# Filling the dummy rows of all later stages in one run during the attention, with a new order of every engine's steps

## The reference

```python
x = x + 0.5 * _L0_ffn_ref(_layernorm(x))     # 8 experts, 128 -> 512 -> 128, gelu, the expert with the top score
x = x + _L0_attn_ref(_layernorm(x))          # conv, then q, k, v with cumulative means, then a 4x MLP with gelu
x = x + 0.5 * _L0_ffn_ref(_layernorm(x))     # the same 8 experts again
x = x + 0.5 * _L1_ffn_ref(_layernorm(x))     # 16 experts, 128 -> 512 -> 128, relu, at most C tokens each
x = x + _L1_attn_ref(_layernorm(x))          # state = a * state + x W_b ; y = layernorm(state W_c)
x = x + 0.5 * _L1_ffn_ref(_layernorm(x))     # the same 16 experts again

# _L1_ffn_ref, its core
C = int(1.25 * T / E)
logits = tokens @ gate_w.T
probs = softmax(logits); expert_idx = argmax(probs)
locations = cumsum(one_hot(expert_idx)) - 1
mask = one_hot(expert_idx) * (locations < C)
dispatch = einsum('tec,td->ecd', sec_mask, tokens)
h = relu(einsum('ecd,edh->ech', dispatch, w1))
ans = einsum('tec,ecd->td', probs * sec_mask, einsum('ech,ehd->ecd', h, w2))
```

## Time and profile before

| | us |
|---|---|
| median of 3 executions | 671.9 (671.17 to 674.94) |
| the profiled execution | 672.23 |
| its span | 670.8 |
| TensorE busy | 617.6 (92%) |
| GpSimd busy | 367.2 (55%) |
| VectorE busy | 448.8 (67%) |
| ScalarE busy | 323.5 (48%) |

### The profile page before, as it was taken

One profiled execution on the slowest core, in us unless ns is written; L12 is line 12 of the kernel. 1 busy time (PEld: TensorE's weight loads), 2 busy tenths in 40 slices (PEclk: granted clock), 3 DMA queues, 4 the chain that ended last, 5 costly groups with the idle time before them and its releaser, 6 DMA issues.

```text
span 670.8 us, 13130 instructions
## 1 busy us (share of the span) xinstructions
PE 617.6 (92%) x3651; PEld 476.8 (71%) x3651; DVE 448.8 (67%) x1882; ACT 323.5 (48%) x1037; POOL 367.2 (55%) x377
## 2 busy tenths in 40 slices
PE   7688899999999999999999799999988987999996
PEld 5547899887867767998998545766744875477773
DVE  5745457886999899854555415778737983477774
ACT  2123558659776555445554105455615731365661
POOL 0647755455220365677557762577760366356776
PEclk8599999999999899999999589999999985999999
DMA  9866676316104032877783514254684411544330
GB/s 266 311 212 194 187 213 202 105 49 201 54 0 83 10 91 61 267 211 201 211 272 99 178 68 104 81 151 141 133 217 142 148 56 51 154 132 142 99 104 15
DMA packets 87031, 94.19 MB, mean 140 GB/s; under 512 B 12156, under 2 KB 65439, under 8 KB 86704
## 3 DMA queue, kind: packets, MB, share of 16 engines
q1 hardware_dynamic: 74400, 74.46, 39.3%
q0 software_dynamic: 10880, 15.07, 6.7%
q10 hardware_dynamic: 1680, 3.82, 1.7%
HBM read 64.42 MB, written 33.76 MB: 146 GB/s over the span
## 4 chain that ended last, share of the span: by engine, by line
PE 63%; DVE 10%; DMA 8%; POOL 6%; issue 5%; ACT 3%; SPq 3%; ACTq 0%; DVEq 0%
PE ps L835 10%; PE ps L827 10%; PE ps L907 6%; PE ps L900 6%; PE ps L882 4%; PE ps L932 4%; PE ps L784 4%; PE ps L745 4%; POOL y L1624 3%; PE ps L849 3%; PE ps L875 3%; POOL xs L1620 2%; PE ps L945 2%; PE ps L817 2%; DMA X<-y 1%
## 5 line engine op out<-in xcount | busy, mean ns | idle before, releaser
L1620 POOL DMA_INDIRECT xs<-X,IDX x128 | 125.8, 982 | 102.9 <-issue 64.1
L1513 ACT ACTIVATE ht<-ps,CL 128x128 f32<-128x128 f32 x336 | 93.0, 379 | 84.6 <-PE ps L827 84.4
L1624 POOL DMA_INDIRECT y<-yt,xi x84 | 83.1, 989 | 48.9 <-DVE yt L1253 33.5
L827 PE MATMUL ps<-xt,w1s 128*128 128x128 f32 x672 | 86.3, 277 | 1.8 <-DVE xt L1247 0.8
L835 PE MATMUL ps<-W,ht 128*128 (+1 forms) x672 | 85.0, 277 | 2.1 <-ACT ht L1513 1.9
L835 PEld LDWEIGHTS ps<-W,ht 128*128 128x128 f32 x672 | 80.0, 192 | 4.4 <-issue 4.2
L827 PEld LDWEIGHTS ps<-xt,w1s 128*128 128x128 f32 x672 | 80.0, 192 | 3.8 <-DVE xt L1247 2.4
L1611 POOL TENSOR_TENSOR sma<-sma,MH 128x4 f32<-128x4 f32 (+1 forms) x24 | 30.6, 1278 | 71.4 <-DVE sma L962 65.1
L932 PE MATMUL ps<-MT,KC 128*128 128x512 f32 x118 | 58.2, 648 | 1.6 <-DVE IDX L1227 1.2
L1570 ACT ACTIVATE hb<-ps 128x320 f32<-128x320 f32 x64 | 26.7, 428 | 51.1 <-PE ps L900 50.8
L1563 ACT ACTIVATE w1s<-x,SE 128x128 f32<-128x128 f32 (+1 forms) x66 | 27.4, 483 | 43.7 <-DVE SE L1356 43.6
(11 more groups left out here) (214 smaller groups left out, 1309.7 us busy)
## 6 DMA issues: line engine op xcount, KB each, us to landing
w1s<-in_w SPq DMA_DIRECT2D x84, 256.0 KB
W<-in_w1x SPq DMA_DIRECT2D x17, 512.0 KB, 4.9
wx<-in_w1x SPq DMA_DIRECT2D x15, 512.0 KB, 4.9
X<-y SPq DMA_DIRECT2D x24, 256.0 KB, 4.7
xs<-ZX SPq DMA_DIRECT2D x32, 185.0 KB
xi<-xs SPq DMA_DIRECT2D x84, 66.0 KB, 3.0
x<-xs SPq DMA_DIRECT2D x22, 148.0 KB, 2.2
xs<-ZB SPq DMA_DIRECT2D x2, 1320.0 KB, 8.5
```

The lines of the kernel that those rows point to most:

```text
L827: r = e.matmul(ps[TILE_BANKS[i % n]][:, c * P:(c + 1) * P], W1[i % NW1][:, c * P:(c + 1) * P], XTT[i % NX][:, :], start=True, stop=True)
L1513: r = e.activation(HT[i % NHT][:, c, :], ps[TILE_BANKS[i % len(TILE_BANKS)]][:, c * P:(c + 1) * P], ACT.Gelu, bias=CL[:, bass.ds(r0 * 4 + ...
L1620: return e.indirect_dma_start(dst, bass.IndirectOffsetOnAxis(ap=IDX[:, n:n + 1], axis=0), X[:, n, 0:w], None, bounds_check=hi, oob_is_err= ...
L1624: return e.indirect_dma_start(dst, bass.IndirectOffsetOnAxis(ap=ix, axis=0), src, None, bounds_check=hi_home, oob_is_err=False, engine_sem ...
```

## The change

`FILL_AFTER` lets all eleven fills go out once one, two or three chunks have left the attention, and SyncE's list has them in one row ahead of the loads of the second layer's first tile. All other lists are written in a new order too. TensorE's list loses three `heat` steps (10 to 12) and three `warm` steps (28, 42 and 58). No other step is added or removed.

```diff
-FILL_AFTER = [("aout", 1 + n // 2) for n in range(len(FILL_GROUPS))] + [("aout", n) for n in (3, 3, 4, 4)] + [("edown", n) for n in (2, 4, 6, 8)]
+FILL_AFTER = [("aout", 1) for n in FILL_GROUPS] + [("aout", n) for n in (2, 2, 2, 2, 3, 3, 3, 3)]
...
     "sp": """
...
-tw.36 tw.37 tw.38 tw.39 tw.40 yload.3 yload.4 yload.5 yload.6 yload.7 fill.0 fill.1 fill.2 fill.3 fill.4 tw.41 fill.5 tload.41 tload.42 tload.43
...
+tw.36 tw.37 tw.38 tw.39 tw.40 yload.3 yload.4 yload.5 yload.6 yload.7 wload.0 fill.0 fill.1 fill.2 fill.3 fill.4 fill.5 fill.6 fill.7 fill.8 fill.9
+fill.10 tw.41 tload.41 tload.42 tload.43 tload.44 tload.45 tload.46 tw.42 tw.43 tw.44 tw.45 tload.47 tload.48 tload.49 tw.46 tw.47 tload.50 tw.48
```

More of the change, by code:

```diff
@@ L228 @@
-eup.49 eup.50 eup.51 eback.11 eturn.13 edown.12 eturn.14 eup.52 eup.53 eup.54 eup.55 eback.12 eup.56 eup.57 eturn.15 edown.13 eup.58 eup.59 eup.60
-eback.13 edown.14 eup.61 eup.62 eup.63 eback.14 edown.15 eback.15 warm.29 warm.30 warm.31 warm.32 warm.33 warm.34 warm.35 warm.36 warm.37 warm.38
-warm.39 warm.40 warm.41 warm.42 rturn.0 rB.0 rturn.1 rturn.2 rB.1 rB.2 rC1.0 rC1.1 rC2.0 rC1.2 rC2.1 rC2.2 pturn.21 rturn.3 rturn.4 pscore.24 pturn.22
-pturn.23 rB.3 rB.4 qrank.8 pscore.25 rturn.5 pscore.26 rC1.3 rC1.4 rturn.6 qrank.9 rC2.3 rC2.4 rB.5 rB.6 pturn.24 qrank.10 pturn.25 pscore.27
@@ L232 @@
-pscore.28 rC1.5 rturn.7 rC1.6 qrank.11 rC2.5 qrank.12 rC2.6 rB.7 pturn.26 pturn.27 pscore.29 rC1.7 pscore.30 qrank.13 rC2.7 qrank.14 pturn.28
-pscore.31 qrank.15 warm.43 warm.44 warm.45 warm.46 warm.47 warm.48 warm.49 warm.50 warm.51 warm.52 warm.53 warm.54 warm.55 warm.56 warm.57 warm.58
-eturn.16 eup.64 eup.65 eturn.17 eup.66 eup.67 eup.68 eup.69 edown.16 eup.70 eup.71 eback.16 eturn.18 edown.17 eup.72 eup.73 eturn.19 eback.17 eup.74
-eturn.20 eup.75 eup.76 eup.77 edown.18 eup.78 eup.79 eback.18 eturn.21 edown.19 eup.80 eup.81 eup.82 eback.19 eup.83 eup.84 eup.85 edown.20 eturn.22
@@ new lines @@
+eback.8 eturn.11 edown.9 eup.43 eup.44 eup.45 eup.46 eup.47 eback.9 eturn.12 edown.10 eup.48 eup.49 eback.10 edown.11 eup.50 eup.51 eturn.13 eback.11
+edown.12 eup.52 eup.53 eturn.14 eup.54 eup.55 eup.56 eup.57 eturn.15 eback.12 edown.13 eup.58 eup.59 eback.13 eup.60 eup.61 edown.14 eup.62 eup.63
+eback.14 edown.15 eback.15 warm.29 warm.30 warm.31 warm.32 warm.33 warm.34 warm.35 warm.36 warm.37 warm.38 warm.39 warm.40 warm.41 rturn.0 rturn.1
+rB.0 rturn.2 rB.1 rB.2 rC1.0 rC1.1 rC2.0 rC1.2 rC2.1 rturn.3 pturn.21 rturn.4 rC2.2 pscore.24 pturn.22 rB.3 rB.4 qrank.8 pturn.23 pscore.25 pscore.26
@@ new lines @@
+rC1.3 rC1.4 qrank.9 rC2.3 rturn.5 qrank.10 rC2.4 rturn.6 rB.5 pturn.24 rB.6 pturn.25 pscore.27 pscore.28 rC1.5 rC1.6 rturn.7 qrank.11 qrank.12 rC2.5
+rC2.6 rB.7 pturn.26 pscore.29 pturn.27 rC1.7 rC2.7 pscore.30 qrank.13 qrank.14 pturn.28 pscore.31 qrank.15 warm.43 warm.44 warm.45 warm.46 warm.47
+warm.48 warm.49 warm.50 warm.51 warm.52 warm.53 warm.54 warm.55 warm.56 warm.57 eturn.16 eturn.17 eup.64 eup.65 eup.66 eup.67 eup.68 eup.69 eup.70
+eup.71 edown.16 eturn.18 eback.16 edown.17 eturn.19 eup.72 eup.73 eturn.20 eup.74 eup.75 eup.76 eup.77 eback.17 eup.78 eup.79 edown.18 eup.80 eup.81
@@ new lines @@
+egate.28 estat.31 eout.27 ex.30 erelv.58 ey.28 erelv.59 enm.31 egate.29 eout.28 erelv.60 ex.31 ey.29 erelv.61 egate.30 egate.31 eout.29 ey.30 erelv.62
+erelv.63 eout.30 ey.31 eout.31""",
+    "act": """
+cenc.0 pstd.0 table.0 tri.0 pcopy.0 pcopy.1 pcopy.2 pcopy.3 pcopy.4 bulk.0 pstd.1 pstd.2 hb2.0 tgelu.0 tgelu.1 tgelu.2 tgelu.3 bulk.1 tgelu.4 tgelu.5
+tgelu.6 tgelu.7 table.1 tgelu.8 tgelu.9 tgelu.10 tgelu.11 tgelu.12 tgelu.13 tgelu.14 tgelu.15 tgelu.16 tgelu.17 tgelu.18 tgelu.19 tgelu.20 tgelu.21
@@ L325 @@
+ehome.24 epow.29 ehome.25 epow.30 ehome.26 epow.31 ehome.27 ehome.28 ehome.29 ehome.30 ehome.31""",
 }
```

233 lines of the change are left out of this document (113 added, 120 removed).

## The result

| | before | after |
|---|---|---|
| median | 671.8 us (20 runs, 666.5 to 676.6) | 676.3 us (20 runs, 671.6 to 683.0) |
| the profiled execution | 672.23 (span 670.8) | 674.1 (span 672.7) |
| TensorE busy | 617.6 us | 613.2 us |

The ratio is 1.0076, with a 95% interval of 1.0054 to 1.0099. The change makes the kernel slower by 0.8%, some 5 us, and I had forecast 663.5 us, faster. A few executions ran in a slower state of the chip (one of the twenty of after, three of the twelve of `t_heat`, and the one of `t_vector` that its trace shows); they are in the medians and not in the ratios.

The account below looks back on a forecast made before the run. TensorE bounds tiles, attention and experts; GpSimd's sends bound the 16-expert routing. Terms -2.6 - 1.2 - 2.35 - 0.6 - 1.1 - 0.8 = -8.65 from 672.23 gave 663.6, stated as 663.5 us, range 656.5 to 671.0.

Parts of the forecast that it names:

- GpSimd's gap: First 16-expert routing: GpSimd's 2.65 us wait before a send shrinks to 0.30, -2.35 us (bounds 0 and -2.35).
- second layer tiles: Second layer: TensorE's 1.16 us wait for a tile, behind fill DMAs, goes; -1.2 us (bounds -2.3 and +1.2).
- First tiles: First layer's start: MT moved, heat steps dropped, table loads later; -1.1 us in sum (bounds -2.9 and +3.5).
- The table load on the path: Program start: a table load now waits for the statistics, moving ranks, first sends and first tile load 1.28 us later.
- the rule: Trainium skill: each table change costs a 1.38 us drain beside the 1.28; the sum would be 1 to 3 us higher.
- `MT`'s move: First tiles: MT's load behind the fourth gelu removes a TensorE stall, -1.9 us, and pushes other loads aside later, +0.5.
- The slower rival: First tiles: without heat the clock falls to its lower level over 44 to 60 us, +7 to +11, 677 us; chance 0.07.
- The fills in the attention: Attention: 32 fill DMAs in place of 12 cost nothing, covered by TensorE's attention work.
- The fills as a whole: Fills moved: -2.6 us at the first 16 experts and -1.2 ahead of the second layer's tiles.
- the clock in the attention: Attention, 222 to 230 us: a 512-column product between 8-column score products lessens the clock dip; -0.8 us (bounds 0 and -1.7).
- the Exp table's load: Start of the 16 experts: this load moves into the warm products, -0.6 us (bounds 0 and -1.3).
- The second routing: Recurrence and second routing, reordered on all engines: 0 us in all (bounds -4.2 and +3.0).

Follow-up runs that it names:

- t_heat: Kernel before with fills moved and the new order through the first layer's tiles, but heat steps 10 to 12 put back; 674.1 us, ratio 0.9993.
- t_vector: Kernel before with fills moved and new order through the first layer's tiles, but VectorE's normalisation of tile 10 later; 671.7 us, ratio 0.9984.
- s_tiles2_old: Changed kernel with the old order on all engines from tile 48 of the second layer to its last tile; 671.9 us, ratio 1.0018.
- t_mt_later: Kernel before with fills moved and new order through the first layer's tiles, but RW and MT loads behind the eighth gelu; 683.3 us, ratio 1.0160.
- t_tables: Kernel before with fills moved and new order through the first layer's tiles, but Sqrt and Gelu table loads in old places; 672.6 us, ratio 1.0003.
- t_mt: Kernel before with fills moved and new order through the first layer's tiles, but RW and MT loads ahead of the first gelu; 674.6 us, ratio 1.0027.
- b_fills: Kernel before with only the fills moved, all eleven in one row ahead of the second layer's first tile loads; 668.2 us, ratio 0.9948.
- b_weights78: Kernel before with only tile 78's weight load moved behind four token loads of the next layer and two of tiles; 673.6 us, ratio 1.0011.
- b_mt_later: Kernel before with fills moved and the RW and MT loads behind the fourth tile's gelu; 670.1 us, ratio 0.9961.

## Why the prediction was wrong

The stages, by the ends of certain steps. "One trace" is the profiled execution of after less that of before; "all traces" is the mean over those whose kernel has the new order in the stage (4 to 8) less the mean over those with the old one (7 to 15). The trace of `t_vector` is left out, and in the first two rows so are those in which `MT` or a table load stands elsewhere.

| stage | forecast | one trace | all traces |
|---|---|---|---|
| start to first normalisation of a tile | -1.0 | -2.9 | -3.1 |
| from there to the end of the first layer's 41 tiles and their loads | -0.1 | +1.7 | +5.0 |
| attention, to the first send of the second layer | -0.8 | -1.8 | -0.1 |
| second layer, to the first send of the next | -1.2 | +5.2 | +4.0 |
| first to ninth send of that layer | 0 | +2.1 | +0.1 |
| ninth to last send (GpSimd's gap) | -2.35 | -2.3 | -2.8 |
| last send to the first result of the 16 experts | -0.6 | -0.1 | 0.0 |
| first 16 experts | -2.6 | -0.7 | -1.5 |
| recurrence and second routing | 0 | -1.4 | -1.2 |
| last 16 experts | 0 | +2.0 | +1.7 |

(In the row of the first 16 experts, "all traces" has the fills out against in, whatever the order.) The column "one trace" adds up to 1.8 us with the rounding, for 1.9 between the two spans; the medians are 4.6 apart, and the rest is not seen in single executions.

*What failed* is the step "second layer tiles", -1.2 with bounds of -2.3 and +1.2. It rested on the one wait that the trace of before has there, and asked what the new order does to it. It did not ask what the new order puts in front of each load and each result. The new order has three things there. The weight load of tile 78 is behind five token loads (0.5 to 2.3 us on the way to the first send). The results of tiles 69 to 71 come within 1.3 us (334.0 to 335.3; before 335.2 to 337.8), since VectorE comes to the first of them only behind three normalisations, and GpSimd takes 1.28 for each scatter: the last one, which the token load waits for, goes out 1.8 us behind its result in all four traces with this order and 0.6 behind it in all sixteen with the old. And from that scatter to the token load it is 3.2 to 3.6 us in these four traces and 2.0 to 2.3 in those sixteen. Why is open: three scatters go out 1.28 us apart in both orders, and the DMA share between the last of them and the token load is 0.74 in after and 0.59 before. Together that is 2.8 to 4.9 us, ahead of a chain (loads, ranks, sends) that nothing covers. `s_tiles2_old` bears it out as a whole: with the old order there the stage is 112.2 us from first send to first send, like before's 111.9, for 114.6 to 117.1 in the new one. The other traces with the old order there have 110.7 to 112.5, but `t_mt_later` has 114.6, with a wait of TensorE of 2.38 us at 318.9 that the order does not explain; the stage has longer executions in either order. The last two parts are read from the traces and were not tried by themselves.

*First tiles* (-1.1, bounds -2.9 and +3.5; the first two rows of the table): the bounds held what happened, the value did not. That the one trace has -1.2 is luck, -2.9 and +1.7 where I had -1.0 and -0.1; over all traces it is +1.9. The table load on the path costs its 1.28 us: the first send comes at 21.1 to 21.5 us in ten traces of the new order, and at 19.8 before and 20.0 in `t_tables`. On the 1.28 itself the row was right against the rule: 10.88 + 1.28 ends at 12.16 and the next activation runs at 12.17; the same at 43.16. The drain of some 1.38 us, in the Trainium skill ("ScalarE: Activation LUTs", "What ACT_TABLE_LOAD costs"), shows in neither row. The first tile's tokens went out at 38.45 and not at 39.15, and took 1.8 us to their use and not 3.0, the median of all such loads, with nothing beside them (5.8 us with `MT` beside them, in `t_mt`). `MT`'s move gave the 41 tiles 2.9 us in one pair of traces in the old order and 0.4 in the other, for my -1.4. What I had wrong was that the new order on VectorE would leave it so, and half of the reason that I gave for a lower clock: I put it on the missing heat steps alone, and the table load behind the first up product, which leaves TensorE idle when it has just begun, has a part in it.

*The slower rival* at 0.07 had this mechanism (the clock falls over the first tiles; it named 0.8 as the point from which it decides, and the traces have 0.76 to 0.89). It is a part of the loss and not all of it: at 0.76 to 0.89 over 16 us the clock costs 16 x 0.11 to 0.24 = 1.8 to 3.8 us, less what the waits hide, and not the 7 to 11 that I had for all 16 us at the lower level. In the profiled execution of after, with 0.85, its own condition is not met. No rival had the second layer's tiles.

*Right:* GpSimd's gap, to 0.1 us in one trace. The fills in the attention cost nothing: in the old order the DMA share over 150 to 205 us rises from 0.23 to 0.50, and the attention takes 87.1 us with them in `b_fills` and 87.0 with them elsewhere in `b_weights78` (before, with the dip, 88.4). The fills as a whole, 3.5 us by the ratio for my 3.8, though at the 16 experts the traces show only 1.5. *Wrong in its cause:* the clock in the attention. The dip (0.95 over 205 to 240 us) is in three traces, `before` and `b_mt_later` with the old order and `s_tiles2_old` with the new one, and costs 1.3 to 1.6 us in each (88.3 to 88.5 us for the stage, against 86.6 to 87.2 in the others); in all other traces the clock there is 1.00. It comes and goes from one execution to the next, and the row of 8-column products that I held responsible does not decide it. *Wrong without harm:* the Exp table's load moved off the start of the 16 experts gives nothing (11.5 us from the end of the last send to VectorE's first result in both orders), so it was covered; by TensorE's queued products, I suppose, which no run shows. The second routing holds no gap at all in the new order: from the first to the last send it is 40.8 us in eight of eight traces, where the old has 41.4 to 45.7, and the recurrence gives 1.7 of that back. The last 16 experts are 1.7 us longer; why was not looked into.
